# Attention stage of a fused block kernel: row maximum of the next pair moved ahead in each step, with exponentials, inverse and residual additions

## The reference, cut to what matters

```python
# 64 batches of 64 tokens, 512 channels
q = x @ Wq; k = x @ Wk; v = x @ Wv
attn = jax.nn.softmax(jnp.einsum('btd,bTd->btT', q, k) * scale, axis=-1)
attn_out = jnp.einsum('btT,bTd->btd', attn, v) @ Wp + bp
cms_out = jax.nn.gelu(attn_out @ cW1 + cb1, approximate=False) @ cW2 + cb2
cms_out = cms_out + target_embed
concat = jnp.concatenate([attn_out, cms_out], axis=-1)
modifier = jax.nn.gelu(concat @ mW1 + mb1, approximate=False) @ mW2 + mb2
out = jnp.clip(x + cms_out + modifier, 0.0, 1.0)
# then an adapter chosen per batch: down, gelu, up, residual, layer norm, gamma, beta
```

## Time and profile before

| what | value |
|---|---|
| median of 2 runs | 2178.12 us (2177.88 to 2178.36) |
| the profiled execution | 2179.99 us, its span 2178.4 us, 1.6 around it |
| granted TensorE clock, mean | 0.981 of 2.4 GHz |
| PE busy | 2052.2 us, 94% of the span |
| DVE busy | 1435.5 us, 66% |
| ACT busy | 965.6 us, 44% |
| the chain that ended last | PE 81%, DVE 9%, SPq 3%, ACT 3%, issue 3% |
| a 128x512 matmul of the large stages, mean | 390 ns |

### The profile page before, as it was taken

One profiled execution on the slowest core, in us unless ns is written; L12 is line 12 of the kernel. 1 busy time (PEld: TensorE's weight loads), 2 busy tenths in 40 slices (PEclk: granted clock), 3 DMA queues, 4 the chain that ended last, 5 costly groups with the idle time before them and its releaser, 6 DMA issues.

```text
span 2178.4 us, 28646 instructions
## 1 busy us (share of the span) xinstructions
PE 2052.2 (94%) x9372; PEld 1691.6 (78%) x9373; DVE 1435.5 (66%) x2701; ACT 965.6 (44%) x1953; POOL 76.6 (4%) x144
## 2 busy tenths in 40 slices
PE   7899999999799999999889999999889999999797
PEld 6678878887678878888668878887668878888686
DVE  6676685555676776556676685556677685564887
ACT  4554443333454453333454443333454444333564
POOL 0000000000000000000000000000000000000122
PEclk9999999999899999999899999999999999999999
DMA  4111131113221231114211222114211131112644
GB/s 165 49 49 53 55 116 59 59 46 138 68 68 40 68 116 59 39 49 155 68 49 59 68 88 61 56 58 153 70 49 59 47 108 59 59 58 78 201 130 113
DMA packets 107967, 171.08 MB, mean 79 GB/s; under 512 B 11646, under 2 KB 71553, under 8 KB 104257
## 3 DMA queue, kind: packets, MB, share of 16 engines
q1 hardware_dynamic: 98672, 126.19, 18.5%
q0 software_dynamic: 9168, 43.26, 5.9%
HBM read 141.62 MB, written 27.79 MB: 78 GB/s over the span
## 4 chain that ended last, share of the span: by engine, by line
PE 81%; DVE 9%; SPq 3%; ACT 3%; issue 3%; DMA 1%; DVEq 0%; POOL 0%; ACTq 0%; POOLq 0%
PE y L1521 17%; PE y L1523 17%; PE y L1522 17%; PE x L1521 10%; PE x L1523 9%; PE x L1522 9%; SPq L418 1%; ACT p_exp L716 1%; SPq L419 1%; DVE xk_lo L1210 1%; DVE a_forms L1146 1%; DVE f L1141 1%; SPq L427 1%; DVE s_sb L1197 1%; DMA h_tile<-wp 0%
## 5 line engine op out<-in xcount | busy, mean ns | idle before, releaser
L1003 DVE TENSOR_TENSOR w_lo<-w_blocks,w_hi 128x512 fp32r<-128x512 f32 (+1 forms) x476 | 255.0, 560 | 69.5 <-ACT w_hi L614 69.5
L614 ACT CAST w_hi<-w_blocks 128x512 fp32r<-128x512 f32 (+1 forms) x476 | 236.5, 515 | 138.7 <-PE y L1523 85.4
L1521 PE MATMUL y<-h_hi,w_hi 128*128 128x512 f32 x512 | 199.5, 390 | 5.9 <-DVE w_lo L1039 5.9
L1521 PE MATMUL x<-h_hi,w_hi 128*128 128x512 f32 x512 | 199.5, 390 | 5.9 <-DVE w_lo L1039 5.9
L1523 PE MATMUL x<-h_hi,w_lo 128*128 128x512 f32 x512 | 199.2, 389 | 0.0
L1523 PE MATMUL y<-h_hi,w_lo 128*128 128x512 f32 x512 | 199.2, 389 | 0.0
L1522 PE MATMUL x<-h_lo,w_hi 128*128 128x512 f32 x512 | 199.2, 389 | 0.0
L1522 PE MATMUL y<-h_lo,w_hi 128*128 128x512 f32 x512 | 199.2, 389 | 0.0
L1521 PE MATMUL x<-a_forms,w_hi 128*128 128x512 f32 x448 | 175.6, 392 | 18.8 <-ACT f L672 8.3
L1521 PE MATMUL y<-a_forms,w_hi 128*128 128x512 f32 x448 | 174.9, 390 | 6.8 <-DVE f L1097 6.8
L1082 DVE TENSOR_TENSOR h_lo<-f,h_hi 128x512 fp32r<-128x512 f32 x256 | 171.4, 686 | 12.8 <-ACT f L672 12.5
(11 more groups left out here) (239 smaller groups left out, 4252.2 us busy)
## 6 DMA issues: line engine op xcount, KB each, us to landing
w_blocks<-w1m SPq DMA_DIRECT2D x128, 256.0 KB, 3.6
w_blocks<-w1c SPq DMA_DIRECT2D x64, 256.0 KB, 3.2
w_st<-w2c SPq DMA_DIRECT2D x64, 256.0 KB, 3.3
w_st<-w2m SPq DMA_DIRECT2D x64, 256.0 KB, 3.7
zs<-z_by_batch SPq DMA_DIRECT2D x68, 128.0 KB, 2.1
xk_st<-xk POOLq DMA_DIRECT2D x32, 256.0 KB, 3.0
cms<-f SPq DMA_DIRECT2D x32, 256.0 KB, 2.8
z_cms<-cms POOLq DMA_DIRECT2D x8, 1024.0 KB, 6.2
```

What stands on the lines that cost most here:

```text
L614: nc.scalar.copy(w1_hi[:, w % RING, cols], src).then_inc(w1_hi_s, 1)
L1003: nc.vector.tensor_tensor(w1_lo[:, w % RING, cols], src, f32(w1_hi[:, w % RING, cols]), ALU.subtract).then_inc(w1_lo_s, 1)
L1521: nc.tensor.matmul(ps, w[0], x[0], start=first, stop=False, skip_group_check=more)
```

## The change

On VectorE, `row_max` of the next pair is the first thing in a step (but for p = 3, where it stays at the end, and p = 7, which has no next pair), `inverse` stands after `split_pt` (for p = 4 before it), and `split_y`, `query` and the rest follow. On ScalarE, `softmax` of the next pair stands between `split_pt` and `split_y` (for p = 4 before `split_pt`), `normalise_p` after `split_y`, and `attended1(s, 0)` moves from the start of step 4 to its end. `softmax` gets one more wait, on `pn_s`. The residual additions 0 and 1 of the preceding tiles move ahead of the first `row_max` of the stage, 2 and 3 to steps 0 and 1, and the clips from steps 3 to 6 to steps 1, 2, 4 and 5. TensorE, GpSimd and SyncE keep their order.

```diff
@@ ScalarE @@
             def softmax(m):
 
                 act.wait_ge(nmx_s, m + 1)
+                if m:
+                    act.wait_ge(pn_s, m)
...
                     m = m0 + p
+                    split_xk(m)
                     if p == NP:
-                        attended1(s, 0)
-                    split_xk(m)
+                        softmax(m + 1)
                     split_pt(m)
+                    if p + 1 < 2 * NP and p not in (NP - 1, NP):
+                        softmax(m + 1)
                     if p and p != NP:
                         for h in range(2):
                             split_y(m - 1, h)
-                    if p == NP - 1:
+                    if p + 1 < 2 * NP and p != NP - 1:
+                        normalise_p(m + 1)
+                    if 0 < p < NP:
                         query(s, DC + p)
...
@@ VectorE @@
                 split_x(2 * s + 1, DC - 1)
+                if s:
+                    z2_sum(s - 1, 0)
+                    z2_sum(s - 1, 1)
                 row_max(m0)
                 inverse(m0)
                 query(s, DC)
                 for p in range(2 * NP):
                     m = m0 + p
+                    if p + 1 < 2 * NP and p != NP - 1:
+                        row_max(m + 1)
+                    split_xk(m)
                     if p == NP:
-                        attended1(s, 0)
-                    split_xk(m)
+                        inverse(m + 1)
                     split_pt(m)
+                    if p + 1 < 2 * NP and p not in (NP - 1, NP):
+                        inverse(m + 1)
                     if p and p != NP:
                         split_y(m - 1)
...
-                    if s and p in (1, 2):
-                        z2_sum(s - 1, 2 * p - 2)
-                        z2_sum(s - 1, 2 * p - 1)
-                    if s and p in (3, 4, 5, 6):
-                        z2_clip(s - 1, p - 3)
+                    if s and p < 2:
+                        z2_sum(s - 1, 2 + p)
+                    if s and p in (1, 2, 4, 5):
+                        z2_clip(s - 1, (1, 2, 4, 5).index(p))
```

More of the change, by code:

```diff
@@ L782, in attention @@
                             split_y(m - 1, h)
-                    if p == NP - 1:
+                    if p + 1 < 2 * NP and p != NP - 1:
+                        normalise_p(m + 1)
+                    if 0 < p < NP:
                         query(s, DC + p)
+                    if p in (NP - 1, 2 * NP - 1):
                         for h in range(2):
                             split_y(m, h)
-                    if p + 1 < 2 * NP:
+                    if p == NP - 1:
                         softmax(m + 1)
                         normalise_p(m + 1)
[L790 to L795, removed]
+                    if p >= NP:
                         attended1(s, p - NP)
@@ L1292, in attention @@
                     m = m0 + p
+                    if p + 1 < 2 * NP and p != NP - 1:
+                        row_max(m + 1)
+                    split_xk(m)
                     if p == NP:
-                        attended1(s, 0)
-                    split_xk(m)
+                        inverse(m + 1)
                     split_pt(m)
+                    if p + 1 < 2 * NP and p not in (NP - 1, NP):
+                        inverse(m + 1)
                     if p and p != NP:
                         split_y(m - 1)
+                    if 0 < p < NP:
+                        query(s, DC + p)
+                    if p in (NP - 1, 2 * NP - 1):
+                        split_y(m)
                     if p == NP - 1:
-                        query(s, DC + p)
-                        split_y(m)
-                    if p + 1 < 2 * NP:
                         row_max(m + 1)
                         inverse(m + 1)
[L1305 to L1309, removed]
+                    if p >= NP:
                         attended1(s, p - NP)
```

## The result

| | before | after |
|---|---|---|
| median | 2178.12 us | 2148.28 us (2145.84, 2150.73) |
| ratio, 95% interval | | 0.9859 (0.9829 to 0.9889) |
| profiled execution, its span | 2179.99, 2178.4 us | 2150.73, 2149.1 us |
| mean granted clock | 0.981 | 0.989 |

The kernel is faster by 1.4%, 30 us, where 36 were forecast: within 2%, and inside the range. Five further runs of the changed kernel gave a median of 2144.74 us (first experiment); the profiled execution here is the slowest of the seven.

What follows compares the result with a forecast made beforehand. TensorE was held to lose twice in attention: 40.8 us waiting for `p_norm` and `pt_hi_lo`, then running at half clock. Gains 10.6 + 3 x 9.8 = 40, less 4 for the clock, gave 2178.1 - 36 = 2142 us, range 2131 to 2162.

Steps and rivals of the forecast that it cites:

- The walk: Attention stages, step by step from start-to-start times at full clock: 10.6 us gained in the first, 9.8 in each other.
- The named waits: TensorE's attention waits after the change: `p_norm` near zero from 29.3 us, `pt_hi_lo` 3 and `split_y` some 5 a stage.
- The residual additions: Two additions (1.20 us) ahead of a stage's first `row_max`: no gain by themselves; 1.2 us leave steps 1 and 2.
- the rest, about 8, is mostly time at half clock: Second stage: of 9.9 us gained, about 2 from waits, about 8 mostly from half-clock time that would go.
- the term of 4 us for the clock: Allowance for clock falls left in the attention stages, at most 1.7 us each; seven would cost 12.
- one fall, 1.7, in the range: A clock fall coming or going at one of the eight stage boundaries: 1.7 us either way, inside the range.
- 40 - 4: Whole kernel: 40 us gained in four attention stages at full clock, less 4 for the clock, gives 36.
- Slower: Rival: `y` cast behind exponentials that wait for `nmx` delays each value product's second half; 2228 us, chance 0.02.
- The clock falls as often as before: Rival: three falls a stage, up to 1.7 us each, take 20 of the 40 us; 2158 us, chance 0.2.

Runs made afterwards that it cites:

- first experiment: The changed kernel timed again in five rounds with no edit: median 2144.74 us, ratio 0.983 to 0.9857 against the kernel before.
- more on TensorE: Changed kernel plus three unused 128x512 matmuls ahead of the value products of steps 1, 2, 5 and 6: 2146.06 us against 2144.74.
- second profile: Profile of the unedited changed kernel when it was timed again in five rounds, taken of the run at 2142.49 us.
- `y` first: Changed kernel with ScalarE's casts of `y` ahead of the exponentials in steps 1, 2, 5 and 6: 2134.77 us against 2144.74.
- reordered kernel: Changed kernel with `y` casts before exponentials, additions and `weight_sums` between `row_max` and `inverse`, other additions and clips earlier: 2134.47 us; with unused matmuls 2127.66.

## Why the prediction was right, and where it was not

*The walk held.* It gave transpositions 2 to 7 of the second stage as offsets of 9.2, 14.4, 23.1, 26.9, 32.4 and 38.0 us. They came at 9.3, 14.6, 23.3, 28.0, 33.5 and 38.6 in that stage and at 8.9, 14.1, 22.9, 26.8, 32.5 and 38.1 in the next. The end was forecast at 45.4 and came at 46.5 and 46.0; the first stage at 42.4 and came at 44.1. It was built from VectorE's and ScalarE's start-to-start times. That TensorE's own work does not set the pace is what "more on TensorE" shows; VectorE's does for some 40% of what is added to it, and ScalarE's part is left by elimination.

*The named waits.* Forecast: `p_norm` zero, `pt_hi_lo` 3 us a stage, `split_y` 5 a stage. Measured: zero, 3.0, and 3.3. VectorE's wait for `p_exp` fell from 30.5 us in 32 waits to 9.1 in 12.

*The residual additions* were priced at nothing themselves, with the gain leaving steps 1 and 2. Put back they cost 2 to 4 us in all, and moved alone they gain nothing; that the gain hangs on the early row maximum was not said.

*The clock was mis-sized, and its reason was wrong.* Two statements failed. First, of the 9.9 us of the second stage "the rest, about 8, is mostly time at half clock". In the rows some of it looks right: half-clock time in the four stretches fell from 51 to 3.4 us. But PE's busy time fell by 18.7 and its waits for the attention's inputs by 18.2, which is 4.7 and 4.6 a stage, and not 8 and 2. (The waits of the earlier trace rows add up to 10.5 and those of the walk to 9.5, so that its own gain from waits was 1. And the fall of the earlier trace rows begins at 564.4, inside the wait of 2.15 that ends at 565.94, and not behind it.) And the first stage of the kernel before at full clock took 52.2 in place of 53.0. The slow matmuls filled time in which TensorE would otherwise have waited for VectorE; holding the clock without changing the order gave 0.9 us, and changing the order, with the clock held too, gave 8.9. The total came out because the walk never used this split.

Second, the term of 4 us for the clock, falls at 1.7 each inside the stages. Inside, the one fall of the first profile cost at most 0.1, and of the five of the second one cost 1.2. The loss came outside and in the first profile alone, 7.0 us, of which 5.1 by more falls at boundaries and amid the products, for which the prediction had allowed one fall, 1.7, in the range. The sum was 40 - 4; measured it is 36.3 (the walk was 3.7 too fast) less 7.0, which is 29.3, and 34.3 plus 3.3 in the second profile. That the stages gave 36.3 where 36 was the sum is luck: the walk's error stands against a term for falls that did not come there.

*The Trainium skill's rule* is that time at the low level costs about one half of it (TensorE: Matmul & The Clock Gate, Terms). It is met amid the products, where TensorE sets the pace: the fall at 800.0 cost 1.7 us of its 3.4. At the start of a product stage it comes out lower: the 3.40 us at 0.50 between 124.10 and 127.50 cost 1.3. By the rule, as an estimate, 10.2 us in the first stage would have cost 5.1; the run shows 0.9.

*The rivals.* "Slower" had the right mechanism, ScalarE's `y` behind the exponentials, at the right place and with a small price: 3.4 to 5.5 us in four stages, as `y` first shows. "The clock falls as often as before" did not happen in the stages (51 us to 3.4). Outside it did get worse in the first profile (six falls in place of two), which none of the rivals had, and better in the second (one).

## What to carry to other kernels

Read which engine idles least in a stage before pricing TensorE's waits. Here the gain was idle time of VectorE: its waits for the exponentials, the query cast and ScalarE's evacuations of `attended1` fell by 38.8 us in all, and the stages by 36.3. Half-clock time of a TensorE that waits for others must not be added to its waits, for here most of it lay in the same hole. When two in-order engines feed each other, put the small result that the other waits for ahead of the bulk work, and cast what is already there first. Unused matmuls in waits paid here directly ahead of a part where TensorE alone sets the pace (6.8 us in the reordered kernel, 2.0 and not clear of the spread in the changed one); in the attention steps of the kernel before they merely moved the fall to a worse place.

## What the runs showed of the hardware

The same waits are followed by a fall in one execution and not in another. Third stage, start of the products, the changed kernel and then the kernel before:

```profile
1088.99 0.47 PE L1526 MATMUL x<-a_forms,w_hi 128*128 128x512 f32 x1 [0.90 <-ACT p_copy L652]
...
1094.34 0.47 PE L1526 MATMUL x<-a_forms,w_hi 128*128 128x512 f32 x1 [1.66 <-DVE f L1099]
...
1099.39 0.47 PE L1526 MATMUL x<-a_forms,w_hi 128*128 128x512 f32 x1 [2.07 <-ACT f L672]
```

```profile
1114.89 0.47 PE L1521 MATMUL x<-a_forms,w_hi 128*128 128x512 f32 x1 [0.90 <-ACT p_copy L652]
...
1120.24 0.47 PE L1521 MATMUL x<-a_forms,w_hi 128*128 128x512 f32 x1 [1.66 <-DVE f L1097]
...
1125.29 0.47 PE L1521 MATMUL x<-a_forms,w_hi 128*128 128x512 f32 x1 [2.07 <-ACT f L672]
```

The waits and the distances between them are the same to 0.01 us. After the first there was a fall at 1100.3, after the second none. So some 1.3 us at such a place can come or go with nothing else changed around it, and the runs of one kernel spread accordingly (2142.5 to 2150.7 us over the changed kernel's seven). What decides it was not settled.
